# A graph network on one core: attention in aligned blocks of 1024 edges, maxima by a segmented scan

## The reference, cut to what matters

```python
h = jnp.maximum(_layernorm(x), 0.0)
x = x + _L0_gnn_ref(h, ...)            # edge MLP, sum by src, node MLP
h = jnp.maximum(_layernorm(x), 0.0)
# one attention layer, done twice
h = (x @ W).reshape(n, heads, ch)
alpha_src = jnp.sum(h * a_src, -1); alpha_dst = jnp.sum(h * a_dst, -1)
e = alpha_src[src] + alpha_dst[dst]
e = jnp.where(e > 0, e, 0.2 * e)
m = segment_max(e, dst); ex = exp(e - m[dst]); s = segment_sum(ex, dst)
out = segment_sum(h[src] * (ex / (s[dst] + 1e-16))[:, :, None], dst) + b
```

## Time and profile before

| what | value |
|---|---|
| median of the timed runs | 11986.09 us |
| span of the profiled execution, first to last instruction | 8886.9 us |
| mean granted clock over the span | 0.771 |
| first attention layer, gathers 4062 to last result 6463 | 2401 us |
| second attention layer, 6532 to 8866 | 2334 us |
| edge MLP, 2480 to 3890 | 1410 us |
| busy share of the span: PE, DVE, ACT, POOL | 69, 69, 55, 70% |

### The profile page before, as it was taken

The page is one execution under the profiler, slowest core; times in us unless marked ns, Lnnn a source line. Parts: engine busy times, 40 slices in busy tenths (PEclk is TensorE's granted clock), DMA queues, the critical chain, the costliest instruction groups (busy, mean ns, idle before and its releaser), DMA issues.

```text
span 8886.9 us, 230055 instructions
## 1 busy us (share of the span) xinstructions
PE 6173.7 (69%) x49885; PEld 5210.5 (59%) x50563; DVE 6168.8 (69%) x25428; ACT 4847.6 (55%) x11854; POOL 6191.5 (70%) x7562
## 2 busy tenths in 40 slices
PE   2466666666599999984666666666646666666665
PEld 2365656556588888873555555545445555656564
DVE  7799833333267676757999999999856666666665
ACT  4133333333245555534777777777647777777775
POOL 0377777777777777735777777777647777777775
PEclk9988888888899999986888888888755555555555
DMA  4233222222232323312222222222421111111114
GB/s 141 52 63 63 62 63 62 63 62 62 61 90 85 86 85 86 85 35 56 55 55 55 55 55 55 56 55 56 47 25 29 29 29 29 29 29 29 29 29 28
DMA packets 990923, 493.64 MB, mean 56 GB/s; under 512 B 830674, under 2 KB 841604, under 8 KB 990276
## 3 DMA queue, kind: packets, MB, share of 16 engines
q0 software_dynamic: 168832, 302.29, 15.6%
q1 hardware_dynamic: 701892, 169.48, 10.2%
q10 hardware_dynamic: 119840, 18.68, 1.3%
HBM read 356.53 MB, written 151.48 MB: 57 GB/s over the span
## 4 chain that ended last, share of the span: by engine, by line
issue 26%; POOL 21%; PE 20%; DVE 15%; DMA 7%; ACT 7%; DVEq 3%; ACTq 1%; POOLq 0%; SPq 0%; another core or an unknown queue 0%
POOL z_s L639 13%; POOL arena L689 8%; DMA arena<-table,arena 6%; PE ps_all L961 5%; PE ps_all L971 5%; ACT arena L825 3%; PE ps_all L984 3%; PE ps_all L981 2%; DVE arena L1494 2%; PE ps_all L1069 1%; ACT arena L857 1%; DVE arena L1580 1%; PE ps_all L993 1%; DVEq L385 1%; DVE ps_all L1232 1%
## 5 line engine op out<-in xcount | busy, mean ns | idle before, releaser
L689 POOL DMA_INDIRECT arena<-table,arena x3616 | 3527.3, 975 | 1421.4 <-issue 963.9
L639 POOL DMA_INDIRECT z_s<-arena x1660 | 1591.9, 959 | 850.8 <-issue 479.6
L1093 PE MATMUL ps_all<-arena 128*128 128x132 f32 (+1 forms) x7232 | 1584.7, 388 | 1.8 <-DVE acc L1597 1.8
L1093 PEld LDWEIGHTS ps_all<-arena 128*128 128x128 f32 x7232 | 1405.9, 288 | 2.7 <-issue 2.6
L1069 PE MATMUL ps_all<-ident_b,arena 128*128 128x128 bf16 x3616 | 465.3, 270 | 1311.8 <-DMA arena<-table,arena 1191.7
L825 ACT ACTIVATE arena<-lanes_b,arena 128x128 bf16<-128x128 bf16 x3616 | 1144.9, 386 | 349.1 <-DVE arena L1467 342.2
L1069 PEld LDWEIGHTS ps_all<-ident_b,arena 128*128 128x128 bf16 x3616 | 282.3, 117 | 1478.6 <-issue 844.4
L1494 DVE TENSOR_REDUCE arena<-ps_all 128x2 f32<-128x1024 f32 x904 | 1098.5, 1215 | 39.0 <-PE ps_all L1110 37.6
L849 ACT ACTIVATE arena<-ps_all 28x512 bf16<-28x512 bf16 (+1 forms) x904 | 527.5, 584 | 956.8 <-PE ps_all L1069 955.8
L744 ACT ACTIVATE arena<-ps_all 18x512 f32<-18x512 f32 x415 | 243.3, 586 | 1211.9 <-PE ps_all L948 1180.1
L1110 PE MATMUL ps_all<-arena,pick 128*128 128x512 bf16 x1809 | 694.6, 489 | 54.6 <-DVE arena L1494 24.3
(11 more groups left out here) (259 smaller groups left out, 15032.7 us busy)
## 6 DMA issues: line engine op xcount, KB each, us to landing
arena<-z_s SPq DMA_DIRECT2D x452, 264.0 KB, 2.7
arena<-table,arena POOLq DMA_INDIRECT x3616
arena<-rec_d SPq DMA_DIRECT2D x1660, 10.0 KB
z_s<-arena POOLq DMA_INDIRECT x1660
rec_d<-in_rec ACTq DMA_DIRECT2D x1, 16160.0 KB, 59.0
arena<-ids_d SPq DMA_DIRECT2D x904, 4.0 KB
arena<-pos_d SPq DMA_DIRECT2D x830, 0.5 KB
arena<-pos_d ACTq DMA_DIRECT2D x830, 0.5 KB
```

The lines of the kernel that those rows point to most:

```text
L639: pool.indirect_dma_start(z_s, bass.IndirectOffsetOnAxis(ap=slot[:, g.slot(SLOTS), u:u + 1], axis=0), z_out[:, g.slot(SLOTS), u, :], None) ...
L689: pool.indirect_dma_start(g_rows[:, r, u * step + CODE_WORDS:(u + 1) * step], None, tables[n], bass.IndirectOffsetOnAxis(ap=ids[:, r, 0, u ...
L1093: mm = pe.matmul(ps[6][:, 0:out_w], a_hot_f[:, g.slot(4), u, :], g_msg[:, g.slot(4), u * out_w:(u + 1) * out_w], start=(u == 0), stop=(u = ...
```

## The change

Attention goes in steps of 1024 edges. A **block** is 1024 edges in plain edge order, two halves of 512, aligned to 1024 whatever the tiles; there are 202. A **visit** is a block together with one destination tile that has edges in it: 202 + 48 = 250 visits per layer. In a visit every edge of the block passes through all stages; edges of other tiles match no lane of the one-hot matrix. Rows are gathered once per block, 8 transfers a block, and stay in a ring of 8 blocks. There is one loop step per visit.

The lane codes, `picks`, the coded rows' transposes and the 512-column products go. In their place DVE copies the gathered shares (`gathered_shares`), PE transposes them to one row per half and head (L1138), DVE scans each row along the 512 edges with a running maximum that restarts at the first edge of every node (`scan_shares`, L1571), PE transposes the result back (L1150), DVE keeps the value at a node's last edge in the half (`segment_ends`, L1581), and PE moves it to the node's lane by a product with the one-hot matrix in f32, 8 products as wide as the heads (L1173). The restart flags are worked out once, during the edge MLP (`edge_flags`), and stored to DRAM; ACT loads them per visit, two transfers (L877). Pipeline depths and rings are shorter: `a_hot`, `a_hot_f` and `turned` hold 4 visits, `g_msg` holds 2. ACT now makes `a_hot_f` in the same stage as it copies `turned` (stage 1 rather than 6), and makes the one-hot matrix after that.

The core of the diff (line numbers in this text below are of the changed kernel where they name its new code):

```diff
+HALVES = 2
+AU = HALVES * U
+BLOCK = HALVES * GE
+BLOCKS = STORED // BLOCK
+VISITS = BLOCKS + NT - 1
+RING = 8
@@ SP, POOL
-                    for u in range(U):
+                    for u in range(AU):
+                        if u == 2 and k.back(1).exists():
+                            landed(k.back(1))
                         pool.indirect_dma_start(
...
@@ ACT, once before the edge MLP
+            act.dma_start(node_of.rearrange(by_edge, u=U), ids_d[1:2, :].rearrange("a (q p u) -> p (a q) u", p=P, u=U)
+                          ).then_inc(S("nodes_in"), 16)
+            act.dma_start(next_of[:, 0:LINEAR // P].rearrange(by_edge, u=U),
+                          ids_d[1:2, 1:LINEAR + 1].rearrange("a (q p u) -> p (a q) u", p=P, u=U)).then_inc(S("nodes_in"), 16)
...
+            def store_firsts():
+                act.wait_ge(S("firsts_known"), 1)
+                act.dma_start(firsts_d[0:1, :], ident_b[0:1, 1:2]).then_inc(S("firsts_out"), 16)
+                act.dma_start(firsts_d[1:STORED + 1, :].rearrange("(q p u) w -> p q (u w)", p=P, u=U), first_flag.rearrange(by_edge, u=U)
+                              ).then_inc(S("firsts_out"), 16)
@@ ACT, one step, in this order
+                    g = of(-1)
...
+                        load_flags(g)
+                    g = of(4)
...
+                        act.wait_ge(S("logit_step"), g.done(LOGIT_STEPS))
...
+                    g = of(1)
...
+                        act.wait_ge(S("turned"), g.done())
...
+                        act.activation(turned[:, g.slot(4), :], ps[(4, 7)[g.slot(2)]].bitcast(BF16), ACT.Copy).then_inc(S("turned_copied"), 1)
                         if g.back(4).exists():
                             act.wait_ge(S("a_summed"), g.back(4).done())
+                        act.activation(a_hot_f[:, g.slot(4)], a_hot[:, g.slot(4)], ACT.Copy).then_inc(S("a_hot_f_ready"), 1)
+                    g = of(0)
...
+                        for u in range(AU):
+                            act.activation(lane_gap[:, g.slot(2), u, :], lanes_b, ACT.Square, bias=neg_lane[:, g.slot(4), u:u + 1]
...
+                        act.activation(a_hot[:, g.slot(4)], lane_gap[:, g.slot(2)], ACT.Relu, scale=-1.0, bias=1.0
@@ PE, one step, in this order
+                    g = of(1)
...
+                        pe.wait_ge(S("a_hot_ready"), g.done())
+                        for u in range(AU):
+                            mm = pe.transpose(bank[:, u * P:(u + 1) * P], a_hot[:, r, u, :], ident_b)
...
+                        for u in range(U):
+                            mm = pe.transpose(by_u[:, :, u], shares[n][:, r, u, :], ident)
...
+                    g = of(2)
...
+                        pe.wait_ge(S("scanned"), g.done())
...
+                            mm = pe.transpose(ps[1][:, u * k:(u + 1) * k], by_u[:, :, u], ident[0:k, 0:k])
...
+                    g = of(5)
...
                         pe.wait_ge(S("a_hot_f_ready"), g.done())
                         pe.wait_ge(S("msg_ready"), g.done())
                         if g.back(1).exists():
                             pe.wait_ge(S("a_added"), g.back(1).done())
...
+                    g = of(2)
...
+                        pe.wait_ge(S("ends_ready"), g.done())
...
+                                mm = pe.matmul(ps[2][:, a * heads:(a + 1) * heads], a_hot_f[:, g.slot(4), a * U + u, :],
+                                               largest[n][:, g.slot(2), u, a * heads:(a + 1) * heads], start=(u == 0), stop=(u == U - 1))
...
+                    g = of(3)
...
+                        pe.wait_ge(S("max_step"), g.done(MAX_STEPS))
...
@@ DVE
+                    dve.tensor_tensor_scan(running[0:k, r, :], flags[0:k, g.slot(4), :], ps[0][0:k, :], -BIG, ALU.add, ALU.max
+                                           ).then_inc(S("scanned"), 1)
 
                 def attend(of):
...
+                    shifts, logs, adds = new_shifts(of(3)), logits(of(4)), sums(of(6))
+                    for part in (logs, shifts):
+                        next(part, None)
+                    edge_lanes(of(0))
+                    segment_ends(of(2))
+                    for part in (logs, shifts, logs, shifts, adds, logs, shifts, adds, shifts):
+                        next(part, None)
+                    scan_shares(of(1))
...
+                    largest_shares(of(2))
+                    messages(of(4))
+                    gathered_shares(of(0))
```

More of the change, by code:

```diff
@@ L1047, in _ @@
                         mm.then_inc(S("gat_mm"), 1)
-                step = CODE_WORDS + row
+                pe.wait_ge(S("low_step"), 2 * n + 1)
+                pe.transpose(ps[6][0:1, 0:P], low_part, ident).then_inc(S("low_shown"), 1)
+                pe.wait_ge(S("low_step"), 2 * n + 2)
+                pe.matmul(ps[6][:, P:P + 1], ones[0:1, :], low_one, start=True, stop=True).then_inc(S("low_shown"), 1)
                 pe.wait_ge(S("table_ready"), n + 1)
-                pe.wait_ge(S("codes_in"), 1)
                 def attend(of):
@@ new lines, in attend @@
+                        mm.then_inc(S("shown"), 1)
+                    g = of(3)
+                    if g is not None:
+                        pe.wait_ge(S("turned_copied"), g.done())
+                        pe.wait_ge(S("max_step"), g.done(MAX_STEPS))
+                        if g.back(1).exists():
+                            pe.wait_ge(S("logit_step"), g.back(1).done(LOGIT_STEPS))
+                        lk = look[:, g.slot(4), 0:6 * heads].rearrange("p (k w) -> p k w", k=3)
+                        for u in range(AU):
+                            for part in range(3):
+                                mm = pe.matmul(ps[5][:, u * 2 * heads:(u + 1) * 2 * heads], turned[:, g.slot(4), u * P:(u + 1) * P],
+                                               lk[:, part, :], start=(part == 0), stop=(part == 2))
+                        mm.then_inc(S("looked_up"), 1)
@@ L1454, in edge_codes, with edge_lanes @@
+                def edge_lanes(g):
                     if g is None:
                         return
[L1456 to L1461 removed]
```

536 lines of the change are left out of this document (279 added, 257 removed).

## The result

The changed kernel takes 12651.03 us in the median (12647.77 to 12671.05, four runs) against 11976.43 us for the kernel before (11957.84 to 12015.44, four runs): a ratio of 1.056, interval 1.0538 to 1.0583, or 675 us more. The direction was forecast; the size was not: +2059 us were.

What follows compares the result with a forecast made beforehand. The prediction took POOL's gathers (with DVE in the first layer) to bound the old kernel and a ring of waits the changed one: +1045 + 927 + 80 + 7 = +2059 us on 11986, 14045 us, range 12400 to 14600.

Steps and rivals of the forecast that it cites:

- What bounds the kernel before: Attention layers before the change: POOL's four gathers, 5.04 us a step, bound the second; POOL and DVE together the first.
- The ring: Attention visits: waits among PE, DVE and ACT close once per visit; 13.2 us at half clock, 10.0 at full.
- hand-overs: Between engines in a visit: four of 0.04 us, with register work and the loop's branch 0.45 us.
- DVE's own list: DVE's work per attention visit (scans, message, sums, some sixteen operations): about 6.5 us, not too long at full clock.
- The clock: PE in attention: lower level for all of the second layer, mostly the lower level in the first; near 0.5.
- two rivals: PE at full clock in the first layer alone, 13280 us, chance 0.18; in both layers, 12464 us, chance 0.09.
- The layers: Both attention layers, 255 x 13.0 + 13 and 255 x 13.2 + 13 us: +927 in the first, +1045 in the second.
- The flags: ACT's two node-number loads ahead of the edge MLP +80 us (bounds 0 and 350); four DVE passes there +7.
- I keep that part as it is: Whole kernel: the 3099 us by which the median exceeds the profiled span stay unchanged, so 11986 + 2059.
- The range: Whole kernel: 12400 to 14600 us, leaving out the POOL-bound case and the same time.
- the rival with full clock in both layers: PE at full clock in both attention layers, by the skill's rule: +162 + 229 + 87, 12464 us; chance 0.09.
- the forecast's own range: Whole kernel, for the forecast case (chance 0.56) alone: 13600 to 14500 us.

## Why the prediction was right in its mechanism and wrong in its size

- **What bounds the kernel before** (POOL in the second layer, POOL and DVE in the first): right, by the run with half its gathers.
- **The ring**: right in every link, and near in length. At half clock 12.4 us a visit, and 15.6 to 16.1 once in eight, against 13.2 forecast: 8 visits take 103.5 us between the starts of their sums, 12.9 each. The longer visit is the end of a round on DVE (last section), 0.5 us a visit, for which the sum had only a share of 0.45 us; without it the ring was forecast 0.8 us too long. Piece by piece: PE's transposes from L1130 to the end of L1150 2.5 us (2.9), DVE from there to L1694's end 1.6 (1.6), L1161 3.65 (3.9), ACT from L906 to L921's end 4.5 (4.35), hand-overs 0.2 (0.45). In the first layer visits of mostly 12.8 us against 13.0. DVE's own list, put at 6.5 us a visit, keeps it busy for 4.1 to 4.7, which changes nothing, as it bounds neither.
- **The clock**: right. 0.57 and 0.50, and not the full clock of two rivals.
- **The layers**: from the first gather of one to the first gather of the next, and from there to the end of the span, 3338 and 3269 us in the quick condition against 2478 and 2356: +860 and +913, where +927 and +1045 were forecast.
- **The flags**: too large. +80 for the transfers and +7 for DVE's passes were forecast; the first gather comes 27 us later in all (4090 against 4063), half of which is the MLP, 1438 for 1424 us. An issue of 95 us on ACT's queue did not occur; the term was nearest its lower bound.
- Quick against quick the sum is **+1800 us measured, +2059 forecast**: 67 and 132 too many in the layers, 60 for the flags.
- **The step that failed**: "The median of the runs is 3099 us above the span; I keep that part as it is." It was not a constant outside the span but time inside the stages, and the change alters it: in the layers the holds cost the kernel before 2217 us and the changed one 1082. The changed kernel issues 1616 gathers a layer for 1808, too small a difference to halve the loss; what differs more is where the late instructions fall. In the kernel before DVE's pauses make POOL wait (661 of 2000 us), and POOL bounds it; in the changed one they fall mostly into waits that DVE had anyway (852 us of 2000 quick, 901 held). 2059 - 259 (the forecast's excess in the quick condition) - 1135 (holds) gives 665 of the 675 measured; the rest is not accounted for.
- **The range**: 12651 us lies inside 12400 to 14600, and that is luck. The lower end was set by the rival with full clock in both layers (12464), and the clock did not rise; the forecast's own range, 13600 to 14500, was missed. By the terms named for it (350 us for the flags, 3% on each visit) the upper end comes to some 14520, not 14600.
- The prediction had the warning in its own numbers: a time 35% above the span of the profile means that the profile is not one of the executions timed. Nothing then says which stages hold the rest, and a range that stands on "as it is" is too sure: two bounds were due, the 3.1 ms kept, and the 3.1 ms shared out over the stages that the change rewrites.

## What to carry to other kernels

Before a sum is made against a profile, compare its span with the times; where they differ by more than a per cent, the missing time needs a place, and a term of its own with both ends. When a step becomes longer than the resource that it was built to spare, look for the ring: four waits, each harmless, closed a loop of 12.4 us of which no engine's list has more than 9.9, and one more PSUM bank and another order on ACT took 1468 us out of 10562. A delay of one engine costs most where another waits for it and it for that one, and least where the delayed engine has a wait in each step that swallows it.

## What the hardware showed that was not expected

- **Other engines' instructions come late while POOL issues rows of eight indirect transfers**, in one condition of the chip: steps of 0.70 us on SP and PE, and 8.4 us on DVE, which goes on some 1.6 us after the last of the row. The condition adds a third to the kernel before (8.90 to 11.98 ms), and halving the gathers, so that rows are of four, removes it from the changed layers (3716 to 3151 us).
- **PE at half clock without a pause**: 2413 of 2420 us busy, at a granted clock of 0.50. The Trainium skill (TensorE: Matmul & The Clock Gate, "Part 1: The HAM clock gate") says that the throttled clock is the default and that sustained activity releases it. If activity means busy time, this trace does not agree. With 128 columns in place of 1 in the same number of products, the one thing changed on PE, the clock in that layer was 0.60 for 0.50, at a smaller busy share (2381 of 3630 us for 2504 of 3686, both held).
- **The end of a round on DVE.** With eight visits to a round the changed kernel has this once in eight visits, quick:

```profile
8029.11 0.16 DVE L1654 TENSOR_TENSOR arena<-arena,ps_all 128x8 f32<-128x8 f32 x1 [3.98 <-issue]
```

With four visits the same place shows this, and the page's instruction queue 66 packets in place of 379:

```profile
8028.10 0.16 DVE L1655 TENSOR_TENSOR arena<-arena,ps_all 128x8 f32<-128x8 f32 x1 [1.19 <-issue]
```

```profile
q14 instruction: 66, 0.54, 0.0%
```

In both a register load stands in the pause (1.1 and 0.8 us); between the branch and the next instruction there are 2.8 us with eight visits and 0.3 with four. The short bodies are not fetched again, as the packets show, and twice as many branches cost less than half as many: 137 us in all. The Trainium skill (Runtime: NRT & Kernel Launch, "Instruction fetch mechanics") says that a taken branch to code outside of what the engine holds must wait for a fetch; the trace agrees, with 3.98 us for a body of 418 DVE instructions and 1.19 us for one of 217.
